# Cross attention: probabilities transposed as two 64-row halves on two row tiles into two banks, in four groups of up to four key blocks

## The reference, cut to what matters

```python
def _L1_xattn_ref(queries, keys, values, mask, Wq, bq, Wk, bk, Wv, bv, Wo, bo):
    ...  # H = 16 heads of HD = 32
    q = split_heads(queries @ Wq + bq)
    k = split_heads(keys @ Wk + bk)
    v = split_heads(values @ Wv + bv)
    scores = jnp.einsum('bhqd,bhkd->bhqk', q, k) / jnp.sqrt(jnp.float32(HD))
    scores = jnp.where(mask, jnp.float32(-1000000000000000.0), scores)
    attn = jax.nn.softmax(scores, axis=-1)
    ctx = jnp.einsum('bhqk,bhkd->bhqd', attn, v)
    ctx = ctx.transpose(0, 2, 1, 3).reshape(b, sq, d)
    return ctx @ Wo + bo
```

## Time and profile before

| | us |
|---|---|
| median of 3 runs | 3736.45 (3735.98 to 3738.56) |
| the profiled execution, whole | 3735.18 |
| its span, first to last instruction | 3733.4 |
| TensorE busy, share of the span | 3148.7 (84%) |
| its weight loads | 2448.1 (66%) |
| VectorE | 2135.5 (57%) |
| ScalarE | 1085.3 (29%) |

### The profile page before, as it was taken

How to read it: one execution, slowest core, us unless ns; L and a number is a source line. 1 busy time by engine, 2 the same in 40 slices (tenths; PEclk the granted TensorE clock), 3 DMA queues, 4 the chain that set the end, 5 groups by cost and what they waited for, 6 DMA issues and landing times. The chain is left out here.

```text
span 3733.4 us, 51743 instructions
## 1 busy us (share of the span) xinstructions
PE 3148.7 (84%) x21798; PEld 2448.1 (66%) x21804; DVE 2135.5 (57%) x3185; ACT 1085.3 (29%) x1680; POOL 387.2 (10%) x110
## 2 busy tenths in 40 slices
PE   6997885999899999999999999999947766369644
PEld 3444674777678888888888888888835322158512
DVE  4224324344436656655555556566554899854597
ACT  2222122222234434433333334344310000023354
POOL 0001001000000000000000000000011677430041
PEclk9998997999999999999999999999968988679867
DMA  7883010111121111001111111110020000011200
GB/s 246 282 286 109 1 37 32 51 51 37 65 83 39 39 39 32 17 30 39 39 39 39 38 39 39 39 39 2 1 76 1 0 0 0 0 51 51 101 1 23
DMA packets 100513, 198.70 MB, mean 53 GB/s; under 512 B 14288, under 2 KB 47056, under 8 KB 99552
## 3 DMA queue, kind: packets, MB, share of 16 engines
q1 hardware_dynamic: 100320, 195.89, 15.6%
HBM read 191.68 MB, written 4.19 MB: 52 GB/s over the span
## 5 line engine op out<-in xcount | busy, mean ns | idle before, releaser
L68 PE MATMUL xa_J<-xa_c_hi,xa_wk_hi 128*128 128x402 f32 x1024 | 376.9, 368 | 20.4 <-DVE xa_c_lo L83 20.2
L69 PE MATMUL xa_J<-xa_c_lo,xa_wk_hi 128*128 128x402 f32 x1024 | 354.9, 347 | 0.0
L70 PE MATMUL xa_J<-xa_c_hi,xa_wk_lo 128*128 128x402 f32 x1024 | 354.6, 346 | 0.0
L1311 ACT ACTIVATE xa_kT_hi<-xa_J,cl_bk 128x402 fp32r<-128x402 f32 x256 | 152.3, 595 | 680.3 <-PE xa_J L70 680.3
L68 PE MATMUL xa_J<-xa_wv_hi,xa_c_hi 128*128 128x512 f32 (+1 forms) x832 | 335.6, 403 | 0.0
L1822 PE MATMUL df_S<-df_prod,main_ident 128*128 128x512 f32 x512 | 231.4, 614 | 114.4 <-DVE df_prod L1776 114.4
L69 PE MATMUL xa_J<-xa_wv_lo,xa_c_hi 128*128 128x512 f32 (+1 forms) x832 | 327.3, 393 | 0.0
L70 PE MATMUL xa_J<-xa_wv_hi,xa_c_lo 128*128 128x512 f32 (+1 forms) x832 | 326.8, 393 | 0.0
L1427 DVE SCALAR_TENSOR_TENSOR xa_kT_lo<-xa_J,cl_bk,xa_kT_hi 128x402 fp32r<-128x402 f32 x256 | 162.2, 634 | 228.8 <-ACT xa_kT_hi L1311 228.1
L1450 DVE TENSOR_TENSOR cl_v<-xa_J,cl_bv 128x512 f32<-128x512 f32 (+1 forms) x208 | 142.1, 690 | 248.3 <-PE xa_J L70 228.4
L1433 DVE CUSTOM_DVE_ANT_0 xa_pr<-xa_S,xa_m 128x804 f32<-128x804 f32 x256 | 248.9, 991 | 50.1 <-PE xa_S L1611 49.4
(11 more groups left out here) (402 smaller groups left out, 6293.6 us busy)
## 6 DMA issues: line engine op xcount, KB each, us to landing
bs_rows<-in_ctx SPq DMA_DIRECT2D x48, 1024.0 KB, 7.3
cl_raw<-in_ctx_cols SPq DMA_DIRECT2D x32, 800.5 KB, 4.4
main_x<-in_ctx_cols SPq DMA_DIRECT2D x32, 800.5 KB, 6.5
bs_cols<-in_ctx_cols SPq DMA_DIRECT2D x24, 802.0 KB, 9.1
moe_raw<-in_L_ffn_routed_w SPq DMA_DIRECT2D x24, 512.0 KB, 4.1
diff_raw<-in_L_attn_W SPq DMA_DIRECT2D x16, 512.0 KB, 3.7
bs_cols<-in_ctx_cols SPq DMA_DIRECT2D x8, 796.0 KB, 6.3
bidaf_w_raw<-in_L_xattn_W_qv SPq DMA_DIRECT2D x4, 1024.0 KB, 9.1
```

The source lines that it names most:

```text
L68: pe.matmul(out, w_hi, x_hi, start=first, stop=False)
L69: pe.matmul(out, w_hi, x_lo, start=False, stop=False)
L70: return pe.matmul(out, w_lo, x_hi, start=False, stop=last)
L1311: nc.scalar.activation(kT_hi[:, j * KG:(j + 1) * KG], J[:, bank(b, ("k", g, j)), 0:KG], ACT.Identity, bias=bk_sb[:, g:g + 1]).then_inc(k_h ...
```

## The change

A turn now covers four blocks of keys instead of two: `T_GROUPS` is four groups (4, 4, 4 and 1 blocks) instead of seven. Each transpose of 128 rows of `pr` is made as two of 64 rows, one on each row tile of the array, the first half into bank 0 of `T`, the second into bank 1. ScalarE copies bank 0 of every turn and VectorE bank 1 of every turn, each into its 64 columns of `pT`. A turn waits for both copies of the turn before it, and the result for both copies of the last turn before it starts. The places of the turns in TensorE's order stay those of the pairs of turns before: new turn 0 stands where 0 and 1 stood, new turn 1 where 2 and 3 stood, and so on. The copies stand where the copies of those pairs stood; VectorE has one more, of the tail, behind `low(b, 1, 0)` at the border and ahead of `low(b + 1, 0, 2)` in group 3.

```diff
@@ -1216,9 +1216,8 @@
 
 
 
-    T_GROUPS = [(n, min(n + 2, KT)) for n in range(0, KT, 2)]
+    T_GROUPS = [(n, min(n + 4, KT)) for n in range(0, KT, 4)]
     TG = len(T_GROUPS)
-    ACT_TG, DVE_TG = (TG + 1) // 2, TG // 2
     PARTS = ((0, 2 * KG), (2 * KG, KEYS))
     HALVED = KC // 2
     with ExitStack() as ctx:
@@ -1243,8 +1242,8 @@
             "c_hi_ready", "c_lo_ready", "m_ready", "q_hi_ready", "q_ready"))
         k_made, v_made, k_hi_ready, k_lo_ready, v_stored, scored, masked, max_ready, exp_done, inv_ready, scaled = (s.sem(n) for n in (
             "k_made", "v_made", "k_hi_ready", "k_lo_ready", "v_stored", "scored", "masked", "max_ready", "exp_done", "inv_ready", "scaled"))
-        turned, t_act, t_dve, o_made, o_stored, o_kept = (s.sem(n) for n in (
-            "turned", "t_act", "t_dve", "o_made", "o_stored", "o_kept"))
+        t_act, t_dve, o_made, o_stored, o_kept = (s.sem(n) for n in ("t_act", "t_dve", "o_made", "o_stored", "o_kept"))
+        turned_half = [s.sem("turned_half0"), s.sem("turned_half1")]
         KU, SU, TU = GR * 4, GR * 2 * 2, GR * TG
         CLEARED = 5
 
@@ -1262,10 +1261,15 @@
 
         def copy_wait(engine, b, g, i):
 
-            if i % 2:
-                engine.wait_ge(t_dve, DVE_TG * (GR * b + g) + i // 2 + 1)
-            else:
-                engine.wait_ge(t_act, ACT_TG * (GR * b + g) + i // 2 + 1)
+            engine.wait_ge(t_act, turn_count(b, g, i))
+            engine.wait_ge(t_dve, turn_count(b, g, i))
+
+        def copied(i, half):
+
+            n0, n1 = T_GROUPS[i]
+            r = rows(n1 - 1)
+            to = pT[0:r, n0:n1, :].rearrange("p n (a h c) -> p n a h c", a=2, h=2)[:, :, :, half, :]
+            return to.rearrange("p n a c -> p (n a) c"), T[0:r, half, 0:(n1 - n0) * P].rearrange("p (x c) -> p x c", c=SEQ)
 
         def bank(b, unit):
             return (len(J_UNITS) * b + J_UNITS.index(unit)) % 2
@@ -1329,11 +1333,9 @@
                                              accum_out=rs[:, i:i + 1]).then_inc(exp_done, 1)
 
                 def copy_turned(b, g, i):
-                    act.wait_ge(turned, turn_count(b, g, i))
-                    n0, n1 = T_GROUPS[i]
-                    r = rows(n1 - 1)
-                    nc.scalar.activation(pT[0:r, n0:n1, :], T[0:r, 0, 0:(n1 - n0) * 2 * P].rearrange("p (n c) -> p n c", c=2 * P),
-                                         ACT.Copy).then_inc(t_act, 1)
+                    act.wait_ge(turned_half[0], turn_count(b, g, i))
+                    to, src = copied(i, 0)
+                    nc.scalar.activation(to, src, ACT.Copy).then_inc(t_act, 1)
 
                 def keep_result(b, g):
                     act.wait_ge(o_made, GR * b + g + 1)
@@ -1360,13 +1362,13 @@
                         copy_turned(old, 3, 0)
                     queries_high(b)
                     if b:
-                        copy_turned(old, 3, 2)
+                        copy_turned(old, 3, 1)
                     widen_mask(b)
                     if b:
-                        copy_turned(old, 3, 4)
+                        copy_turned(old, 3, 2)
                     high(b, 1, 0)
                     if b:
-                        copy_turned(old, 3, 6)
+                        copy_turned(old, 3, 3)
                     high(b, 1, 1)
                     if b:
                         keep_result(old, 3)
@@ -1389,20 +1391,20 @@
                         copy_turned(b, g - 1, 0)
                         if load_next:
                             high(b + 1, 0, 1)
-                        copy_turned(b, g - 1, 2)
+                        copy_turned(b, g - 1, 1)
                         if load_next:
                             high(b + 1, 0, 2)
                             high(b + 1, 0, 3)
                         keep_key(b, g, 3)
-                        copy_turned(b, g - 1, 4)
-                        copy_turned(b, g - 1, 6)
+                        copy_turned(b, g - 1, 2)
+                        copy_turned(b, g - 1, 3)
                         if g + 1 < GR:
                             keep_key(b, g + 1, 0)
 
                 last = BATCH - 1
                 exps(last, 3)
                 keep_result(last, 2)
-                for i in range(0, TG, 2):
+                for i in range(TG):
                     copy_turned(last, 3, i)
                 keep_result(last, 3)
 
@@ -1451,9 +1453,9 @@
                         .then_inc(v_stored, 1)
 
                 def copy_turned(b, g, i):
-                    dve.wait_ge(turned, turn_count(b, g, i))
-                    n0, n1 = T_GROUPS[i]
-                    nc.vector.tensor_copy(pT[:, n0:n1, :], T[:, 1, :].rearrange("p (n c) -> p n c", c=2 * P)).then_inc(t_dve, 1)
+                    dve.wait_ge(turned_half[1], turn_count(b, g, i))
+                    to, src = copied(i, 1)
+                    nc.vector.tensor_copy(to, src).then_inc(t_dve, 1)
 
                 def keep_results(b):
                     dve.wait_ge(o_stored, GR * b + GR)
@@ -1483,15 +1485,16 @@
                         normalise(old, 3, 1)
                     keep_key(b, 0, 0)
                     if b:
-                        copy_turned(old, 3, 1)
+                        copy_turned(old, 3, 0)
                     keep_key(b, 0, 1)
                     if b:
-                        copy_turned(old, 3, 3)
+                        copy_turned(old, 3, 1)
                     queries_low(b)
                     if b:
-                        copy_turned(old, 3, 5)
+                        copy_turned(old, 3, 2)
                     low(b, 1, 0)
                     if b:
+                        copy_turned(old, 3, 3)
 
                         dve.wait_ge(o_made, GR * b)
                     keep_values(b, 0)
@@ -1530,14 +1533,15 @@
                         if load_next:
                             low(b + 1, 0, 0)
                         keep_key(b, g, 2)
-                        copy_turned(b, g - 1, 1)
+                        copy_turned(b, g - 1, 0)
                         if load_next:
                             low(b + 1, 0, 1)
-                        copy_turned(b, g - 1, 3)
+                        copy_turned(b, g - 1, 1)
                         mask_scores(b, g, 0, 0)
                         mask_scores(b, g, 0, 1)
                         keep_key(b, g, 3)
-                        copy_turned(b, g - 1, 5)
+                        copy_turned(b, g - 1, 2)
+                        copy_turned(b, g - 1, 3)
                         if load_next:
                             low(b + 1, 0, 2)
                         if g + 1 < GR:
@@ -1547,7 +1551,7 @@
                 last_masks(last, 3)
                 normalise(last, 3, 0)
                 normalise(last, 3, 1)
-                for i in range(1, TG, 2):
+                for i in range(TG):
                     copy_turned(last, 3, i)
                 keep_results(last)
 
@@ -1615,24 +1619,24 @@
                 def turn(b, g, i):
                     if i == 0:
                         pe.wait_ge(scaled, 2 * (GR * b + g) + 2)
-                    if i >= 2:
-                        copy_wait(pe, b, g, i - 2)
-                    elif i == 0 and GR * b + g:
-                        copy_wait(pe, *divmod(GR * b + g - 1, GR), TG - 1)
-                    elif i == 1 and GR * b + g:
-                        pe.wait_ge(o_stored, GR * b + g)
+                        wait_after(pe, o_stored, GR * b + g)
+                    else:
+                        copy_wait(pe, b, g, i - 1)
                     n0, n1 = T_GROUPS[i]
                     for n in range(n0, n1):
                         r = rows(n)
                         for a in range(2):
-                            last = pe.transpose(T[0:r, i % 2, (2 * (n - n0) + a) * P:(2 * (n - n0) + a + 1) * P],
-                                                pr[:, a, n * P:n * P + r], ident[:])
-                    last.then_inc(turned, 1)
+                            at = (2 * (n - n0) + a) * SEQ
+                            for half in range(2):
+                                hs = slice(SEQ * half, SEQ * half + SEQ)
+                                last = pe.transpose(T[0:r, half, at:at + SEQ], pr[hs, a, n * P:n * P + r], ident[hs, hs])
+                                if n == n1 - 1 and a == 1:
+                                    last.then_inc(turned_half[half], 1)
 
                 def result(b, g):
                     if g == 0:
                         pe.wait_ge(v_stored, KT * b + KT)
-                    copy_wait(pe, b, g, TG - 2)
+                    copy_wait(pe, b, g, TG - 1)
                     for i, (n0, n1) in enumerate(T_GROUPS):
                         copy_wait(pe, b, g, i)
                         for n in range(n0, n1):
@@ -1655,18 +1659,15 @@
                     key_tile(b, 0, 1)
                     if b:
                         turn(old, 3, 0)
-                        turn(old, 3, 1)
                     value_tile(b, 0)
                     if b:
```

(21 more changed lines are left out.)

## The result

The changed kernel takes 3759.53 us, median of 4 runs (3756.32 to 3762.31), against 3737.45 (3735.98 to 3738.56) in 4 runs of the kernel before beside it: a ratio of 1.0059, 95% interval 1.0042 to 1.0076. It is 22 us slower. The profiled executions differ by 23.6 us (span 3757.0 against 3733.4), nearly all of it in the cross attention.

The account below looks back on a forecast made before the run. TensorE, busy 1571 of 1591 us in cross attention, was taken as the bound. Per batch +0.53, times 15 is 8.0, with -0.3 and -0.4 at the end: +7.3, forecast 3743 us, range 3727 to 3760.

Parts of the forecast that it names:

- The price of a pair: In every turn, two 64-row transposes side by side take 0.061 us, bounds 0.056 and 0.109.
- The rival of 0.11: In every turn, a pair costs as much as a full transpose, 0.11 us: +68 us, 3805; chance 0.10.
- The change of mode: Around TensorE's turns, entering one costs 0.15 us, leaving it for a key or value tile 0.20.
- The cheap emptying: Around turns, the 0.09 us of emptying falls away: 1.4 us less per batch, -22, 3721; chance 0.10.
- Groups 1 to 3: Turns in these groups of each batch: 0.05, 0.05 and 0.16 us gained, copy waits included.
- The second semaphore wait of a turn is met before the first ends: At the start of each turn on TensorE, the wait for the second copy adds no time.
- The border: Between batches, the old batch's last result waits for VectorE's tail copy and loads 0.79 us later, 15 times.
- The rival without a wait there: At the batch border, the result does not wait for the tail copy: -13 us, 3730; chance 0.08.
- The last group: The last batch's final group, standing alone, shortens from 5.60 to 5.15 us, -0.4.
- Slow copies: Both engines reading `T` at once slows copies by 0.3 us each: 1.2 a batch, 3762; chance 0.10, with the like.

Follow-up runs that it names:

- The reordering: Changed kernel with the third turn moved right behind the first scores and the fourth right ahead of the second scores: 3735.01 us, ratio 0.9994.
- The single semaphore: Changed kernel with both copies of a turn counting up one semaphore, so TensorE waits once, not twice: 3748.58 us, ratio 1.0030.
- The first experiment: Changed kernel with VectorE's small copy of the tail at a batch start put ahead of `low(b, 1, 0)`, not behind: 3749.75 us, ratio 1.0035.
- the tail in one bank: Changed kernel with the 65-row tail turned by two full transposes into bank 0, copied by ScalarE alone: 3727.22 us, ratio 0.9974.
- full rows: Changed kernel with one full transpose per 128-row block in place of two 64-row halves, new grouping kept: 3794.35 us, ratio 1.0159.

## Why the prediction was right or wrong

The direction that I gave the most chance (0.48) held, and the range did, by luck: 3759.53 lies 0.5 us inside its upper end, two of the four runs lie above it, and it is outside the 3736 to 3751 that my sums allowed. The value did not hold: +7.3 us was forecast on the profile, +23.6 came.

- **The price of a pair**: 0.061 forecast, 0.063 measured. The rival of 0.11 has fallen.
- **The change of mode**: turn 0 goes from the last key matmul (start due at 1962.87) to L68's at 1963.71, 0.84 as forecast. The cheap emptying, which would have made it shorter, has fallen. The reordering shows its price from the other side.
- **Groups 1 to 3**: -0.05, -0.05 and -0.16 forecast (the terms as printed give -0.12 for the last), +0.15, +0.16 and +0.08 measured. The step that failed is "The second semaphore wait of a turn is met before the first ends", which I had costed at nothing. Where VectorE's copy is the last, it isn't met, and it is an instruction of its own: the load comes 0.12 behind the copy, not 0.05, and the tiles start staggered. The single semaphore took 0.19, 0.18 and 0.19 away, 0.56 of the 0.65 between forecast and result. The Trainium skill says as much, on the page "Perfetto Trace Analysis", section "Identifying Dependency Chains": an instruction that waits on several engines may have EventSemaphore instructions put ahead of it for the further conditions. The trace agrees, with 51 ns for one. I had not drawn on it.
- **The border**: +0.79 forecast, +0.85 measured, with the wait at L1647 and the tail copy behind L83 where I had them (0.28 for it, as taken). The first experiment and the tail in one bank confirm the cause. The rival without a wait there has fallen.
- **The last group**: -0.4 forecast, +1.3 measured up to its result, and +1.3 in the result. I had counted its rounds at the full clock; the granted clock was 0.50. In the kernel before the window there has this row:

```profile
2698.00:2706.00 8.00, 6.76 (x130) 5.32 (x130) 2.45 (x4) 2.40 (x5) 0.00 (x0) 0.79 0.00 0
```

  The clock had fallen there as well, behind a stop of the same length (4.4 us), but it came back while the turns ran nearly without a gap, and the result had the full clock:

```profile
2700.00:2702.00 2.00, 2.00 (x10) 1.77 (x10) 0.57 (x2) 0.60 (x1) 0.00 (x0) 0.50 0.00 0
2704.00:2706.00 2.00, 1.66 (x104) 1.50 (x104) 0.00 (x0) 0.46 (x2) 0.00 (x0) 1.00 0.00 0
```

  So the risk could be read from the trace. That the longer stops kept the clock down is likely from this comparison, but no run separates it.
- **Slow copies**: have fallen (0.686 and 0.599 against the earlier trace rows).
- **The single stall** of 1.6 us was in no term.

Of the missing 16.3 us, 8.4 are the second wait, 0.9 the border, 3.2 + 0.7 the last batch, 1.6 the stall, and 1.4 are left in the groups.

The change was thus two in one: half rows, worth 1.6 us per batch here, and a grouping that costs 2.9. What half rows are worth hangs on their place: with the turns beside the scores it is 2.6 (0.83 + 0.84 + 0.86 + 0.08).

## What to carry to other kernels

When a buffer of two banks is given up for a larger turn, ask which copy each consumer waits for at its start, and leave a small remainder in the bank that the next consumer doesn't write: that edit, with the full rows and the single wait that went with it, gave 1.87 us per batch, more than the half rows in the same grouping (1.63). Small row tiles pay where they stand beside other work of the same tiling, and a turn between full-row products gives its gain back at both ends. If two engines release one, let them count up one semaphore; and when a wait goes, look for the next copy in the same queue before counting the gain.

## What the runs showed of the hardware that was not expected

- A second wait ahead of a weight load shows as a semaphore instruction of 51 ns, and delays the load by 0.07 us when it is the last to be met. After it the two row tiles of a pair started 33 ns apart, and 16 loads took 0.61 instead of 0.58 us.
- With TensorE stopping about 0.9 us ahead of each turn in the last group, the granted clock stayed at 0.50 (before, with smaller gaps, it was back at 1.00 for the result), and 104 matmuls of the result took 3.00 instead of 1.66 us.
- Single stalls, in which TensorE waited for nothing that the profile shows, lengthened a distance by 0.6 to 6.1 us in the profiled executions of three kernels (after, full rows, reordered), in none of the others. All eight, and a ninth that was caught up, end 2.3 to 2.6 us after the start of a packet of the DMA queue that is marked as instructions (the one at 1697.44 behind a packet from 1695.02 to 1695.95), while such packets come only every 12 to 14 us in the mean. So TensorE was probably waiting for its own instructions; the trace doesn't say for which engine a packet is, and no run tests it. In the two longest TensorE's loads stood for 4.5 and 3.2 us, and behind each the granted clock was 0.50 for 3.4 us; that makes up the rest of their 6.1 and 4.9.
